# A two-part layer on one core: the slots of its four state-space layers are put in another order, and the last tile's down rows are turned one chunk later

## The reference, cut to what matters

```python
# part 1: x is (1, 2048, 512); h is 64 wide; four layers
h = x @ Win.T + bin
for each layer:
    y = silu(layernorm(h, ln1_w, ln1_b))
    y = sconv(y, phazor, last_conv)          # a complex decaying recurrence over the 2048 tokens
    h = h + y * sc_lin
    y = layernorm(h, ln2_w, ln2_b)
    h = h + silu(y @ w1.T + b1) @ w2.T + b2  # 256 wide
x = layernorm(x + layernorm(h, lnl_w, lnl_b) @ Wout.T + bout)
# part 2: gated block, weights looked up in a codebook (8192, 8)
Wg, Wu, Wd = codebook[idx_gate], codebook[idx_up], codebook[idx_down]   # 1376 x 512, 1376 x 512, 512 x 1376
x = layernorm(x + (silu(x @ Wg.T) * (x @ Wu.T)) @ Wd.T)
```

## Time and profile before

| | us |
|---|---|
| median of three runs | 1268.66 (1265.54 to 1270.40) |
| the profiled execution | 1264.5 |
| its span in the profile | 1262.5 |
| PE busy | 1188.8 (94%) |
| DVE busy | 1011.6 (80%) |
| POOL busy | 929.9 (74%) |
| ACT busy | 261.7 (21%) |

### The profile page before, as it was taken

How to read it: one execution, slowest core, us unless ns; L and a number is a source line. 1 busy time by engine, 2 the same in 40 slices (tenths; PEclk the granted TensorE clock), 3 DMA queues, 4 the chain that set the end, 5 groups by cost and what they waited for, 6 DMA issues and landing times.

```text
span 1262.5 us, 16835 instructions
## 1 busy us (share of the span) xinstructions
PE 1188.8 (94%) x5595; PEld 839.3 (66%) x5595; DVE 1011.6 (80%) x2194; ACT 261.7 (21%) x395; POOL 929.9 (74%) x895
## 2 busy tenths in 40 slices
PE   6857998889999999999999999999999999999998
PEld 4533444346777777777777777777777777778876
DVE  3998898878997778888777888778888778888845
ACT  2325777772000000000000000000000000000024
POOL 6777777777777777777777777777777777777710
PEclk8968999989999999999999999999999999999999
DMA  9331211102433223433223433333433333334303
GB/s 202 64 68 37 45 37 39 27 4 53 105 92 87 65 71 80 95 82 92 65 69 79 89 85 81 65 70 86 93 85 87 67 70 79 94 72 88 60 2 133
DMA packets 96971, 93.57 MB, mean 74 GB/s; under 512 B 53549, under 2 KB 57909, under 8 KB 96886
## 3 DMA queue, kind: packets, MB, share of 16 engines
q1 hardware_dynamic: 64692, 83.86, 23.0%
q0 software_dynamic: 28160, 3.66, 8.5%
q10 hardware_dynamic: 4034, 4.98, 1.4%
HBM read 87.53 MB, written 4.90 MB: 73 GB/s over the span
## 4 chain that ended last, share of the span: by engine, by line
POOL 73%; issue 21%; PE 4%; DMA 1%; DVE 0%; ACT 0%; POOLq 0%; SPq 0%; DVEq 0%
POOL stage_down L400 57%; POOL stage_up L389 16%; PE bank L652 2%; PE cand L652 2%; DMA work<-in_L_ffn_idx_up 0%; DMA stage_down<-in_L_ffn_codebook,idx_down 0%; ACT x L505 0%; POOLq L160 0%; DVE chosen L1229 0%; DVE x L1033 0%; PE bank L924 0%; SPq L315 0%; DVE idx_low L1091 0%; DVE idx_low L1092 0%; DVE shift L1239 0%
## 5 line engine op out<-in xcount | busy, mean ns | idle before, releaser
L400 POOL DMA_INDIRECT stage_down<-in_L_ffn_codebook,idx_down x688 | 722.3, 1050 | 209.7 <-issue 209.1
L652 PE MATMUL cand<-one_hot,book 128*128 128x512 f32 (+1 forms) x2432 | 622.7, 398 | 19.0 <-DVE one_hot L1057 19.0
L1057 DVE TENSOR_SCALAR one_hot<-bc,low_of 128x512 fp32r<-128x512 uint16 (+1 forms) x1216 | 512.8, 482 | 99.0 <-PE cand L652 97.3
L652 PEld LDWEIGHTS cand<-one_hot,book 128*128 128x128 f32 x2432 | 449.7, 189 | 187.2 <-DVE one_hot L1057 51.8
L389 POOL DMA_INDIRECT stage_up<-in_L_ffn_codebook,idx_up x192 | 205.6, 1071 | 63.8 <-issue 58.2
L652 PE MATMUL bank<-x1t_hi,w 128*128 128x512 f32 (+1 forms) x704 | 239.1, 396 | 0.0
L1075 DVE SCALAR_TENSOR_TENSOR chosen<-bc,high_of,cand 128x512 f32<-128x512 uint16 (+1 forms) x304 | 220.2, 724 | 21.1 <-PE bank L652 17.9
L652 PEld LDWEIGHTS bank<-x1t_hi,w 128*128 128x128 f32 (+1 forms) x704 | 130.3, 185 | 31.4 <-issue 2.1
L652 PE MATMUL bank<-x1t_lo,w 128*128 128x512 f32 (+1 forms) x352 | 137.7, 391 | 0.0
L598 ACT ACTIVATE prod<-bank 128x512 f32<-128x512 f32 (+1 forms) x44 | 26.3, 599 | 389.4 <-PE bank L652 389.4
L605 ACT ACTIVATE act_hi<-prod 128x512 fp32r<-128x512 f32 x40 | 25.3, 633 | 342.5 <-DVE prod L1033 342.5
(11 more groups left out here) (181 smaller groups left out, 751.8 us busy)
## 6 DMA issues: line engine op xcount, KB each, us to landing
bc<-index_parts SPq DMA_DIRECT2D x272, 256.0 KB, 3.3
stage_down<-in_L_ffn_codebook,idx_down POOLq DMA_INDIRECT x688, 2.7
bc<-index_parts_rest SPq DMA_DIRECT2D x32, 192.0 KB, 3.1
x<-in_L_attn_x ACTq DMA_DIRECT2D x4, 1024.0 KB, 9.8
out_x<-x SPq DMA_DIRECT2D x16, 256.0 KB, 2.0
stage_up<-in_L_ffn_codebook,idx_up POOLq DMA_INDIRECT x192
index_parts<-parts_t SPq DMA_DIRECT2D x20, 32.0 KB, 2.0
w_in<-in_L_attn_W ACTq DMA_DIRECT2D x2, 256.0 KB
```

The lines of the kernel that those rows point to most:

```text
L400: pool.indirect_dma_start(stage_down[k % RING][:, q, j * CS:(j + 1) * CS], None, a["L0_ffn_codebook"], bass.IndirectOffsetOnAxis(ap=idx_do ...
L652: return pe.matmul(dst, lhs, rhs, start=start, stop=stop)
L1057: done = v.tensor_scalar(one_hot[quad % 2][:, q, 0:nw], bc[quad % BCS][:, 0:nw], low_of[:, q:q + 1], None, ALU.is_equal)
```

## The change

In the layer stage the instructions are the same and stand in another order. On PE a slot now begins with its first quad, then come `variance1` and `variance2` side by side, `back`, `rotated`, a second quad if there is one, `spread`, and `mixed` of the item before at the end of the slot. On DVE the slot begins with the one-hots and with the damping of the item before (new function `damp`), `add_mixed` moves behind `u`, and the scan comes last. On ACT `root2` goes ahead of `root1`, and `square1` and `silus` ahead of `square2`. The waits follow the new order. In the end loop `turn_down(FULL, REST)`, with its copies on ACT and DVE, moves from round 0 to round 1, each `down` from round c to round c+1, and the loop on PE and DVE has one round more.

```diff
--- before.py
+++ after.py
@@ -111,6 +111,11 @@
 
         slots = AHEAD_QUADS - EARLY
         return range(EARLY + -(-t * slots // ITEMS), EARLY + -(-(t + 1) * slots // ITEMS))
+
+    def states_through(t):
+
+        last = min(t, ITEMS - 1)
+        return last // NC * (NC - 1) + last % NC
 
     def cand_of(quad):
         return quad % 3 if quad < AHEAD_QUADS else (quad - AHEAD_QUADS) % 3
@@ -541,19 +546,19 @@
 
             kept = 0
             for t in range(ITEMS):
-                root1(t)
                 if t >= 2:
                     root2(t - 2)
+                root1(t)
                 lay = cols[:, t // NC, :]
                 act.wait_ge(s["normed1"], t + 1)
                 if t:
                     act.wait_ge(s["scanned"], t)
                 act.activation(y, xn, ACT.Silu, bias=lay[:, LN1_B:LN1_B + 1], scale=lay[:, LN1_W:LN1_W + 1]).then_inc(s["silu_made"], 1)
+                square1(t + 1)
+                if t >= 2:
+                    silus(t - 2)
                 if t:
                     square2(t - 1)
-                if t >= 2:
-                    silus(t - 2)
-                square1(t + 1)
 
                 act.preload_act_table(ACT.Abs_reciprocal_sqrt)
                 while kept < unit_of(quads_in(t)[0]):
@@ -636,10 +641,11 @@
             for c in range(NC):
                 silu(FULL, REST, c)
                 product_hi(FULL, REST, c)
-                if c == 0:
+                if c == 1:
                     down_hi(FULL, REST)
-                if c >= 2:
-                    out_chunk(c - 2)
+                if c >= 3:
+                    out_chunk(c - 3)
+            out_chunk(NC - 3)
             out_chunk(NC - 2)
             for n in range(TPC):
                 t = (NC - 1) * TPC + n
@@ -847,8 +853,10 @@
 
             def mixed(i):
                 pe.wait_ge(s["damped"], i + 1)
-                if i >= 3:
-                    pe.wait_ge(s["h_made"], i - 2)
+                if i:
+                    pe.wait_ge(s["h_mid"], i)
+                if i >= 2:
+                    pe.wait_ge(s["h_made"], min(ITEMS - NC + 1, i - 1))
                 mm(bank[0][:, :], mix[:, i // NC, :], d).then_inc(s["mixed"], 1)
 
             def variance1(i):
@@ -860,17 +868,15 @@
                 mm(bank[1][:, :], mean_p[0:D, :], sq1[0:D, :]).then_inc(s["var1"], 1)
 
             def variance2(i):
-                t = i + 2
                 pe.wait_ge(s["sq2_made"], i + 1)
-                if t < ITEMS and t % NC:
-                    pe.wait_ge(s["state_kept"], t // NC * (NC - 1) + t % NC)
+                pe.wait_ge(s["state_kept"], states_through(i + 1))
                 if i:
                     pe.wait_ge(s["ff_made"], i)
                 mm(bank[2][:, :], mean_p[D:P, :], sq2[i % 2][D:P, :]).then_inc(s["var2"], 1)
 
             def back(i):
                 pe.wait_ge(s["ff_made"], i + 1)
-                pe.wait_ge(s["h_mid"], min(ITEMS, i + 3))
+                pe.wait_ge(s["h_mid"], i + 2 if i < ITEMS - 3 else ITEMS)
                 if i:
                     pe.wait_ge(s["h_made"], i)
                 for k in range(FK):
@@ -881,32 +887,36 @@
                 pe.wait_ge(s["normed2"], i + 1)
                 pe.wait_ge(s["rs1_made"], min(ITEMS + 2, i + 3))
                 pe.wait_ge(s["rs2_made"], i + 1)
+                pe.wait_ge(s["state_kept"], states_through(i + 2))
                 for k in range(FK):
                     half = slice(k * D, (k + 1) * D)
                     done = mm(bank[1 + k][:, :], w1t[half, i // NC, :], g2[half, :])
                 done.then_inc(s["spread"], 1)
 
+            variance1(0)
             for t in range(ITEMS):
                 quads = quads_in(t)
-                if t % NC:
-
-                    pe.wait_ge(s["scanned"], t)
-                    if t >= 3:
-                        pe.wait_ge(s["ff_made"], t - 2)
-                    mm(bank[2][:, 0:1], turn[:, t // NC, :], g[:, C - 1:C]).then_inc(s["rotated"], 1)
+                candidates(quads[0])
                 if t:
-                    mixed(t - 1)
-                variance1(t)
+                    variance1(t)
                 if t >= 2:
                     variance2(t - 2)
                 if t >= 3:
                     back(t - 3)
-                candidates(quads[0])
+                if t % NC:
+
+                    pe.wait_ge(s["scanned"], t)
+                    if t >= 2:
+                        pe.wait_ge(s["rs2_made"], t - 1)
+                    mm(bank[2][:, 0:1], turn[:, t // NC, :], g[:, C - 1:C]).then_inc(s["rotated"], 1)
+                for quad in quads[1:]:
+                    candidates(quad)
+                add_up(quads[0] - 1)
                 if t >= 2:
                     spread(t - 2)
+                if t:
+                    mixed(t - 1)
                 for quad in quads[1:]:
-                    candidates(quad)
-                for quad in quads:
                     add_up(quad - 1)
 
             def turn_down(k, n):
@@ -949,9 +959,9 @@
                         now.then_inc(s[made], 1)
 
 
-            mixed(ITEMS - 1)
             variance1(ITEMS)
             variance2(ITEMS - 2)
+            mixed(ITEMS - 1)
             back(ITEMS - 3)
             project(0)
             spread(ITEMS - 2)
@@ -1010,13 +1020,13 @@
                         if quads[slot] > AHEAD_QUADS:
                             add_up(quads[slot] - 2)
             add_up(ALL_QUADS - 1)
-            for c in range(NC + 1):
+            for c in range(NC + 2):
                 if c < NC:
                     hidden(FULL, REST, c, 0, 1)
-                if c == 0:
+                if c == 1:
                     turn_down(FULL, REST)
-                else:
-                    for t in range((c - 1) * TPC, c * TPC):
+                if c >= 2:
+                    for t in range((c - 2) * TPC, (c - 1) * TPC):
                         down(FULL, (FULL - 2, FULL - 1, FULL), t, (bank[2][:, :], cand[0][:, :], cand[1][:, :], cand[2][:, :]))
 
         @block.vector
@@ -1251,6 +1261,12 @@
                 v.wait_ge(s["mixed"], i + 1)
                 tt(hc, hc, bank[0][:, :], ALU.add).then_inc(s["h_mid"], 1)
 
+            def damp(i):
+                v.wait_ge(s["scanned"], i + 1)
+                if i:
+                    v.wait_ge(s["mixed"], i)
+                tt(d, g, tab[:, i // NC, :], ALU.mult).then_inc(s["damped"], 1)
+
             def norm2(i):
                 lay = cols[:, i // NC, :]
                 v.wait_ge(s["rs2_made"], i + 1)
@@ -1277,12 +1293,16 @@
             for t in range(ITEMS):
                 l, c = divmod(t, NC)
                 quads = quads_in(t)
+                one_hots(quads[0] + 1)
+                if t:
+                    damp(t - 1)
+                for quad in quads[1:]:
+                    one_hots(quad + 1)
+                if t >= 2:
+                    norm2(t - 2)
                 if c:
                     v.wait_ge(s["rotated"], l * (NC - 1) + c)
                     v.tensor_copy(state[:, :], bank[2][:, 0:1]).then_inc(s["state_kept"], 1)
-                if t:
-                    add_mixed(t - 1)
-                one_hots(quads[0] + 1)
                 v.wait_ge(s["rs1_made"], t + 1)
                 if t < NC:
                     v.wait_ge(s["h_begun"], t + 1)
@@ -1291,34 +1311,31 @@
                 if t:
                     v.wait_ge(s["silu_made"], t)
                 tt(xn, h[:, c * C:(c + 1) * C], rs1, ALU.mult).then_inc(s["normed1"], 1)
-                if t >= 2:
-                    norm2(t - 2)
                 if t >= 3:
                     add_back(t - 3)
+                choose(quads[0])
                 v.wait_ge(s["silu_made"], t + 1)
                 tt(u, y, tab[:, l, :], ALU.mult).then_inc(s["turned_back"], 1)
+                if t:
+                    add_mixed(t - 1)
+                for quad in quads[1:]:
+                    choose(quad)
                 v.wait_ge(s["turned_back"], t + 1)
+                if t:
+                    v.wait_ge(s["damped"], t)
                 if c:
                     v.wait_ge(s["state_kept"], l * (NC - 1) + c)
                 begin = state[:, :] if c else cols[:, l, STATE0:STATE0 + 1]
                 v.tensor_tensor_scan(g, cols[:, l, DECAY:DECAY + 1].to_broadcast([P, C]), u, begin, ALU.mult, ALU.add
                                      ).then_inc(s["scanned"], 1)
-                v.wait_ge(s["scanned"], t + 1)
-                if t:
-                    v.wait_ge(s["mixed"], t)
-                tt(d, g, tab[:, l, :], ALU.mult).then_inc(s["damped"], 1)
-                choose(quads[0])
-                for quad in quads[1:]:
-                    one_hots(quad + 1)
-                    choose(quad)
-
-
+
+            damp(ITEMS - 1)
             for b in range(2):
 
                 v.memset(hn[b][D:D + 1, :], 1.0)
-            add_mixed(ITEMS - 1)
             norm_last(0)
             norm2(ITEMS - 2)
+            add_mixed(ITEMS - 1)
```

(10 more changed lines are left out.)

## The result

The changed kernel takes 1274.76 us (median of 6 runs, 1272.2 to 1276.46), the kernel before 1267.89 beside it (6 runs, 1265.54 to 1270.4): the ratio is 1.0054, 95% interval 1.0038 to 1.0069. So it is slower, by 6.9 us. The two profiled executions lie further apart, at 1276.46 against 1264.5 us, their spans at 1274.7 against 1262.5: the trace of before is 3.4 us under its median, that of after 1.7 over.

The account below looks back on a forecast made before the run. PE and POOL were taken as two bounds ending together: 1264.5 - 0.3 (tile 7) - 0.3 (tile 10) + 2.8 (clock) gave 1266.7 us; allowing for the timed runs, near 1269 us, range 1263 to 1274.

Parts of the forecast that it names:

- Two bounds that meet at tile 7: At turn_down(7) PE meets POOL's gathers with 0.3 us in hand, so an earlier PE wins only 0.3 us.
- The lead: PE leaving the layers about 10 us earlier; the rival that this reaches the end gave 1258.4 us, chance 0.06.
- Layers faster: Layer stage: one-quad slots fall from 8.67 to 7.6 to 8.0 us, and PE leaves about 10 us earlier.
- Clock at tile 7: After PE's new wait of about 9.7 us at turn_down(7) its clock halves, costing 2.8 us, bounds 0 and 3.4.
- End loop: Tile 10's turn_down, one chunk later, no longer waits for gathers: -0.3 us, with 1 us either way for layernorm groups.
- POOL's pace: Layer stage: gathers ahead of turn_down(7) keep their pace under the new DVE order; nought, 1.5 us either way.
- the packed slots slow POOL: Rival, layer stage: tighter slots slow roughly 100 gathers, tile 7 and the end come 5 us later, 1274; chance 0.12.
- the 140 ns: Layer-stage gathers average 1085 ns against 945 in the last 9 us; the difference was read as DVE's doing.
- PE is late, POOL or neither: Cases for timed runs lying above the profiled one, median by 4.2 us: 1266.7, 1270.0 or 1270.9 us respectively.

Follow-up runs that it names:

- n2: Changed kernel with norm2 ahead of damp, last shares of up gathers later, and tile 10's turn_down one chunk later; second run, 1264.41 us, ratio 0.9982.
- h1: Changed kernel with the end loop of the kernel before; 1274.33 us, ratio 1.0046.
- k1: Separate kernel replaying DVE's one-quad slot beside gathers, in three orders and two paces; 1129 and 1144 ns a gather at the old pace, 1231 to 1571 at the new.
- k2: Separate kernel replaying the one-quad slot at ten lengths, eight in the new order and two in the old; mean gather 1389 ns at 8.56 us, 1162 at 8.78.
- m1: Changed kernel with two added DVE copies of bank 0, about 1.0 us together, in one-quad layer slots; 1270.74 us, ratio 1.0028.
- n1: Kernel before, layers untouched, with the last shares of up gathers later and tile 10's turn_down two chunks later; 1267.93 us, ratio 1.0012.
- n3: Changed kernel with only the last shares of up gathers later; 1269.37 us, ratio 1.0030.
- e5: Separate kernel with 12 POOL gathers beside each kind of DVE instruction; 954 ns a gather alone, 1269 beside one-hots.
- the combined kernel: Changed kernel with norm2 ahead of damp, later last up shares and tile 10's turn_down one chunk later; 1263.12 us (0.9958), then as n2 1264.41 (0.9982).

## Why the prediction was wrong

The forecast was 1269 us, no change that can be told. Measured were 1274.76 us, 6.9 more than the kernel before.

- **Two bounds that meet at tile 7: right.** The lead did not reach the end; PE gave it all back in a wait at `turn_down(7)`.
- **Layers faster: right.** The slot, at 7.69, is in the forecast 7.6 to 8.0, with no wait for the silus and the state the next to be late. PE's lead at tile 0 is 7.1 us instead of about 10, and 11.7 in n2, where the clock holds behind the layers. A second fall of the clock, behind the layers, is not in the prediction. In the changed kernel it cost nothing at the end, as PE waited at tile 7 all the same.
- **Clock at tile 7: right.** It fell in the new wait. From the read of tile 7 to that of tile 8 it is 111.48 us, before 109.08: 2.4 us more, 2.8 was forecast. One reading was too selective: an idle time of 3.25 us ahead of 30.6 in the trace of before brought no fall.
- **End loop: right.** No wait at tile 10, and from the read of tile 8 to the end 201.1 us, before 201.7: 0.6 less, where 0.3 was forecast (h1: 1.0046 without the new loop, 1.0054 with it).
- **The step that failed is POOL's pace**, "I put it at nought, with 1.5 us either way". POOL was 10.75 us late at tile 7. The reason given was that DVE's instructions ahead of tile 7 are the same in number, "and so is the time they take from POOL, if the cost goes with them". It does not go with them: for the same DVE instructions in the 15 intervals, 80 gathers were held for 24.1 us, where before 100 had been held for 14.8. A gather that meets an instruction on SBUF waits for its end and then comes back at a point that DVE's rhythm sets, so POOL runs in step with the slot: 6 gathers, at times 7, in 8.67 us, and 5 in 7.69. A slot 11% shorter takes at least 17% fewer. In the 123.4 us between the first and the last scan, the pace of before would have given 88 gathers and there were 80; 8 times 1.40 is 11 us. The replay (k1, k2) shows the step with nothing else running, and for two orders of DVE's instructions. In the kernel m1 shows that the slot's length is a cause: with the new order at 8.51 us a slot takes 6 again, and 6.2 of the 10.75 us are gone. What makes the other 4.5 isn't shown.
- **The rival "the packed slots slow POOL" was the true case**, with its place right, and its price, 5 us, half of what the traces show. I had it at 0.12, because "DVE's work is the same". The trace before could have said otherwise: the 140 ns more per gather are a mean of gathers at 0.94 us and of three, at 1.15, 1.35 and about 1.3 us, that follow one another once in a slot (they start at 157.56, 166.04, 193.73, 202.25 and 213.39). I read the mean and not the pattern.

By the medians the loss is 6.9 us and not 12.2. Part of that is the kernel before. The prediction asked whether its timed runs lie above the profiled one because PE is late, POOL or neither. Its 29 runs beside n1 to n3 speak for PE: time and mean granted clock go against each other, with a correlation of -0.86, and -0.92 in the twelve of n1, where PE is the only bound. What PE loses there by its clock, the changed kernel's PE loses out of its lead. This accounts for 3.4 of the 5.3 us at most; the rest isn't resolved. Profiles of kernels with these layers had means between 96 and 236 us of 1222, 1232, 1200 and 1212 ns, with the old layers 1099 and 1113: all of the new ones are slower, by an amount that varies with the execution. Open is which phase POOL falls into in a given run, and why.

## What to carry to other kernels

A queue on GpSimd that seems to run by its own clock can be in step with VectorE: before a VectorE loop is made shorter, count how many gathers one pass of it takes, and ask whether that whole number survives. Of two bounds that end together, the one that isn't touched by an edit still has to be priced under the edit's new rhythm. And when PE gains a lead that another engine takes back, look for what PE wants from it last, and ask for it later: here the lead paid, by 0.2 to 0.4% against the kernel before, only after tile 10 and the shares of up gathers had moved.

## What the runs showed of the hardware

- An indirect DMA on POOL takes 0.94 us with DVE idle, and as long beside each of the three kinds of DVE instruction with an operand in PSUM that were tried (e5: 943, 942 and 943 ns), and 1.27 us beside one-hots. It can be held more than once: in k2 one was in a scan's way and then in that of four one-hots, and took 2.84 us.
- Products and norm2's form held gathers less when they stood alone (971 and 1046 ns) than in the kernel's mixture (1189 and 1324 by the start of the gather). What holds a gather is the meeting, and rhythm decides how often they meet. (The kernel's two figures are means of 13 gathers each.)
- More waiting on DVE isn't always more room for POOL: in k2 the slot of 8.56 us took as many gathers as that of 7.79.
- The same program can differ by more than the change is worth: the combined kernel waited 5.11 us at tile 10 in one profile and 11.47 in another, and PE's clock fell behind the layers in the first and not in the second.
